# Attention, then routed experts on one core: TensorE's pass regrouped, and x split into f16 parts before its transposes

## The reference

```python
qkv = x @ W_attn + b_attn
q, k, v = jnp.split(qkv, 3, axis=-1)            # 16 heads of 16
scores = jnp.einsum('bhtd,bhsd->bhts', q, k) * scale
scores = jnp.where(causal & (j >= i - 64), scores, -jnp.inf)
out = softmax(scores) @ v
x = layernorm(x + out @ W_proj + b_proj)
...
expert_idx = argmax(softmax(x @ Wr.T))
inter = gelu(x @ W1[expert] + b1[expert])       # 256 -> 1024
y = inter @ Wo + bo + x                         # 1024 -> 256
x = layernorm(x + layernorm(y) * gamma + beta)
```

## Time and profile before

| | us |
|---|---|
| median of 3 runs | 536.47 |
| lowest, highest | 534.67, 536.82 |
| the profiled execution | 537.07 |
| its span (first to last instruction) | 535.3 |
| first transposes of the maxima (pass 0) | 31.95 |
| the same of pass 1, of pass 27, of pass 31 | 42.02, 265.42, 299.76 |

### The profile page before, as it was taken

The page is one execution under the profiler, slowest core; times in us unless marked ns, Lnnn a source line. Parts: engine busy times, 40 slices in busy tenths (PEclk is TensorE's granted clock), DMA queues, the critical chain, the costliest instruction groups (busy, mean ns, idle before and its releaser), DMA issues. The chain is left out here.

```text
span 535.3 us, 24509 instructions
## 1 busy us (share of the span) xinstructions
PE 491.7 (92%) x8576; PEld 434.6 (81%) x8576; DVE 427.2 (80%) x1122; ACT 351.9 (66%) x793; POOL 317.7 (59%) x559
## 2 busy tenths in 40 slices
PE   7799999998999999999977898899999999999980
PEld 6588888877888888888866687788999999999970
DVE  5437978877888888888788647999999989999882
ACT  6246786856686777768676665565676666767850
POOL 8303264535354545546454447777888888888773
PEclk9969999989999999999999899999999999999996
DMA  7797777776877867797762121222235564542100
GB/s 188 210 240 194 216 188 195 206 215 157 216 211 212 234 184 214 210 249 204 199 177 78 52 71 52 71 72 67 66 104 168 194 206 158 170 144 72 50 23 8
DMA packets 90296, 82.28 MB, mean 154 GB/s; under 512 B 36534, under 2 KB 83903, under 8 KB 90050
## 3 DMA queue, kind: packets, MB, share of 16 engines
q1 hardware_dynamic: 86832, 72.26, 49.5%
q0 software_dynamic: 3248, 8.41, 4.6%
q10 hardware_dynamic: 98, 0.04, 0.0%
HBM read 43.50 MB, written 23.55 MB: 125 GB/s over the span
## 5 line engine op out<-in xcount | busy, mean ns | idle before, releaser
L1409 PE MATMUL ps<-v_even,w_hi 128*128 128x128 f16 x1024 | 140.5, 219 | 0.8 <-issue 0.8
L1391 PE MATMUL ps<-wo_hi,ks 128*128 128x256 f16 (+1 forms) x576 | 128.6, 273 | 8.1 <-DVE ks L1087 7.2
L830 ACT ACTIVATE probs<-ps,b1T 128x128 f32<-128x128 f32 (+1 forms) x312 | 85.5, 360 | 67.1 <-PE ps L1409 63.8
L1409 PE MATMUL ps<-v_even,w_lo 128*128 128x128 f16 x512 | 107.9, 219 | 0.0
L1409 PEld LDWEIGHTS ps<-v_even,w_hi 128*128 x1024 | 96.6, 98 | 3.4 <-issue 1.4
L1158 DVE TENSOR_REDUCE mx<-ps 128x4 bf16<-128x512 f32 x128 | 82.6, 683 | 11.9 <-PE ps L1460 11.6
L740 POOL CAST att_hi<-att 128x256 f16<-128x256 f32 x32 | 12.6, 394 | 112.8 <-DVE att L1225 112.8
L1391 PE MATMUL ps<-wo_lo,ks 128*128 128x256 f16 (+1 forms) x288 | 78.5, 273 | 0.0
L1087 DVE TENSOR_TENSOR ks<-probs,ks 128x512 f16<-128x512 f32 (+1 forms) x72 | 69.7, 967 | 8.5 <-ACT ks L837 5.0
L849 ACT ACTIVATE probs<-ps 128x512 f32<-128x512 f32 x128 | 69.5, 611 | 6.7 <-PE ps L1486 3.8
L1509 PE MATMUL ps<-v_odd,probs 128*64 128x17 f32 x1024 | 69.9, 210 | 0.8 <-issue 0.6
(11 more groups left out here) (247 smaller groups left out, 1280.9 us busy)
## 6 DMA issues: line engine op xcount, KB each, us to landing
qk_s<-qk_room SPq DMA_DIRECT2D x32, 256.0 KB, 2.8
w_in<-in_L_ffn_W_dram SPq DMA_DIRECT2D x16, 512.0 KB, 5.7
v_odd<-slots SPq DMA_DIRECT2D x64, 128.0 KB
qs<-qk_s SPq DMA_DIRECT2D x16, 384.0 KB
ks<-qk_s SPq DMA_DIRECT2D x16, 384.0 KB, 5.5
ks<-qk_s SPq DMA_DIRECT2D x32, 144.0 KB
v_even<-v_odd SPq DMA_DIRECT2D x63, 68.0 KB, 3.2
qk_s<-qk_room SPq DMA_DIRECT2D x32, 128.0 KB, 3.0
```

What stands on the lines that cost most here:

```text
L830: last = nc.scalar.activation(g[1 - p][:, ic, n * w:(n + 1) * w], ps_h[1 - p][:, half, col + n * w:col + (n + 1) * w], ACT.Gelu, bias=b1T[ ...
L1391: ins = mm(ps_y[p][0:m], h[p][hs][:, ic, 0:m], wo[ws][:, ic, :], start=n == 0, stop=n == 3 * IC - 1)
L1409: up_ins = mm(ps_h[1 - p][:, half, col + m * w:col + (m + 1) * w], weights(ws, m, k, ic), sT[1 - p][ss][:, k, at], start=k + n == 0, stop= ...
```

## The change

Eight parts:

- On TensorE the output projection and the transposes of x come first, then scores(0) and scores(1), values(0) and the rest (in pass 0 the scores stay first).
- x of the loop (tiles 4 and on) is cut into parts before it is transposed: one pass ahead, ScalarE writes the high f16 part and GpSimd the low one into `part_room`; TensorE makes four f16 transposes of them into bank 4; ScalarE copies both parts out in one instruction. VectorE's `x_low` in the loop goes.
- The tiles `mx` are 128 wide instead of 32, and so is the output of their transposes.
- ScalarE writes the rows of maxima ahead of `v_odd`.
- VectorE computes y and the logits ahead of the maxima, copies att before `router_x`, and does the places ahead of W1.
- W1's halves are two in even passes and none in odd ones, up to pass 28.
- The ranks go to bank 6, but for the last pair, with their wait for v and the router gone; values(0) waits for the places instead.
- Transposes of x no longer wait for the queries and keys of the tile ahead.

```diff
-        mx = [sb(f"mx{k}", [P, P - ALIGNED], bf16) for k in range(2)]
+        mx = [sb(f"mx{k}", [P, P], bf16) for k in range(2)]
...
+        x_part = part_room[:, 0:2 * C].rearrange("p (s c) -> p s c", s=2)
...
+        ps_xT = ps[:, 4, 0:C].bitcast(f16).rearrange("p (s k t) -> p s k t", s=2, k=CC)
...
+        def ps_rank(pair):
+            return ps[:, 6 if pair < TILES // 2 - 1 else 1, 320:320 + 3 * E].rearrange("p (a e) -> p a e", a=3)
...
         def w1_halves(it):
-            halves_at = range(it - 1, it) if it < TILES - 3 else range(2 * it - TILES + 2, 2 * it - TILES + 4)
+            halves_at = range(it - 2, it if it % 2 == 0 else it - 2) if it < TILES - 3 else range(2 * it - TILES + 2, 2 * it - TILES + 4)
...
+                n = it + LEAD + 1
+                if n >= LEAD and a_tile(n):
+                    pool.wait_ge(part_h_done, n - LEAD + 1)
+                    nc.gpsimd.tensor_tensor(x_part[:, 1, :], xin[n % XRING], x_part[:, 0, :], ALU.subtract)\
+                        .then_inc(part_l_done, 1)
                 n = it - 1
                 if a_tile(n):
                     pool.wait_ge(att_done, n + 1)
...
                 for t in turned(it) if it > FIRST else ():
-                    x_high(t)
+                    if t < LEAD:
+                        x_high(t)
+                    else:
+                        act.wait_ge(xT_done, t + 1)
+                        wait(act, v_done, t - 3)
+                        nc.scalar.activation(xT_room[:, 2 * (t % 4):2 * (t % 4) + 2, :],
+                                             ps_xT.rearrange("p s k t -> p s (k t)"), ACT.Copy).then_inc(xl_done, 1)
+                n = it + LEAD + 1
+                if n >= LEAD and a_tile(n):
+                    act.wait_ge(xin_ld[n % 3], 16 * (n // 3 + 1))
+                    nc.scalar.activation(x_part[:, 0, :], xin[n % XRING], ACT.Copy).then_inc(part_h_done, 1)
...
+                cur = a_tile(it)
+                if cur:
+                    act.wait_ge(mxT_done, it + 1)
+                    maxima_rows(0)
+                    maxima_rows(1)
                 if a_tile(it + 1):
                     m = it + 1
                     act.wait_ge(v_done, m + 1)
...
-                maxima(0)
-                maxima(1)
-                for t in turned(it) if it > FIRST else ():
-                    x_low(t)
                 if a_tile(old):
                     dve.wait_ge(proj_done, old + 1)
...
+                maxima(0)
+                maxima(1)
+                for t in turned(it) if FIRST < it < 0 else ():
+                    x_low(t)
...
                 if it == 0:
                     warm(20)
-                scores(0)
+                    scores(0)
+                    scores(1)
                 if a_tile(old):
...
-                    wait(pe, place_done, old // 2)
...
-                scores(1)
                 for t in turned(it):
+                    if t >= LEAD:
+                        pe.wait_ge(part_l_done, t - LEAD + 1)
+                        pe.wait_ge(xl_done, t)
+                        wait(pe, exp_done, 4 * (it - 1) + 1)
+                        for part in range(2):
+                            for k in range(CC):
+                                last = nc.tensor.transpose(ps_xT[:, part, k, :], x_part[:, part, k * P:(k + 1) * P], ident_h[:, :])
+                        last.then_inc(xT_done, 1)
+                        continue
                     pe.wait_ge(xin_ld[t % 3], 16 * (t // 3 + 1))
-                    if t >= LEAD:
-                        pe.wait_ge(qkh_done, t)
-                        pe.wait_ge(qkl_done, t)
...
+                if it != 0:
+                    scores(0)
+                    scores(1)
                 values(0)
```

42 lines of the change are left out of this document (18 added, 24 removed).

## The result

| | before | after |
|---|---|---|
| median, us | 536.64 (534.67 to 538.25, 4 executions) | 547.13 (544.06 to 549.44, 4 executions) |
| profiled execution, us | 537.07 | 549.44 |
| its span, mean granted clock | 535.3, 0.976 | 547.7, 0.942 |
| first transposes of maxima T0, then T1 | 31.95, 42.02 | 33.36, 43.22 |
| T1 to T27 (26 passes) | 223.40 | 231.02 |

The ratio is 1.0166, with an interval of 1.0121 to 1.0212: slower, where 531.0 and faster were forecast, and outside the range of 519.5 to 540. Of the 12.4 us of span, 1.2 are there at T1, 7.6 come in the 26 passes and 3.4 in the last four; the stage behind them is unchanged.

A forecast was written before the change was run, and what follows sets the result against it. TensorE's own length (98% busy) was taken to bound the 26 attention passes. Terms: -6.4 there, -1.2 in the last four passes, +2.1 at the start, sum -5.5 us, median 531.0; forecast 527 to 534, range 519.5 to 540.

The forecast's parts named there:

- Tile shapes and transposes: TensorE's pass: six array-shape changes removed save 0.62 us, f16 transposes of x 0.05; 8.17 falls to 7.50.
- The waits at values(0) and scores(2): TensorE waits 0.30 us for exponentials every pass, 0.24 for a maximum in even ones: passes 7.80 odd, 8.04 even.
- The other 11.0 us are scattered waits that I take to stay: In the 26 attention passes, time beyond 212.4 us of wait-free passes was taken as unchanged: 11.0 us.
- VectorE's chain, worked out for passes with two splits of W1: Even passes: both splits delay the first maximum to T + 5.90, so scores(2) waits 0.24 us; odd passes no wait.
- The last four passes, "-1.2": Last four attention passes: three removed array-shape changes on the path save 0.30 us each pass, -1.2 us.
- The start, "+2.1": Pass -1: ScalarE stands until 25.4 us for tile 4's x, delaying the first maximum and scores(2): +2.1 us, bounds 0 to 4.
- The rival of 545 us, splits of W1 against GpSimd: Even passes: both W1 splits on VectorE collide with GpSimd's work, scores(2) waits 1.08 us more, 13 times: +14.0, 545.0; chance 0.12.
- The full gain, 520: Rival: new waits at values(0) and scores(2) don't arise, TensorE's whole saving arrives: gain 16.5 us, 520.0; chance 0.23.
- The lower end of the range: Whole kernel's time: 519.5 us, described as the middle of the full-gain case, 518 to 526.

The follow-up runs named there:

- mx_first: The changed kernel with VectorE's first two maxima put back ahead of y and the logits: 542.34 us, 1.0107 times the kernel before.
- lock_bad: lock_good with 102 fillers in pass 0 in place of 50, which moves TensorE's instruction fetch boundaries: 551.11 us, 1.032 times the kernel before.
- lock_good: fix4 with small TensorE fillers, 50 in pass 0 and more in odd passes, to hold instruction fetch boundaries in place: 534.51 us, 0.9925 times the kernel before.
- wo_odd: The changed kernel with Wo's four pieces split in passes 15 to 21 instead of 14 to 20: 540.79 us, 1.0044 times the kernel before.
- fix4: The changed kernel with the edits of mx_first and wo_odd, and W1 halves one each in passes 27 and 28: 539.19 us, 1.0049 times the kernel before.
- thin_before: The kernel before with loads of stacked queries and keys cut to an eighth from pair 4 on: 528.45 us, 0.9867 times the kernel before.
- w1_single: The changed kernel with one half of W1 split in every pass instead of two in even passes: 541.08 us, 1.0066 times the kernel before.
- thin_fix4: fix4 with loads of stacked queries and keys cut to an eighth from pair 4 on: 529.16 us, 0.9916 times the kernel before.
- after_again: The changed kernel run once more, nothing altered: 546.0 us, 1.021 times the kernel before.
- thin_after: The changed kernel with loads of stacked queries and keys cut to an eighth from pair 4 on: 534.57 us, 0.9992 times the kernel before.

## Why the prediction was wrong, point by point

- **Tile shapes and transposes** ("TensorE's own pass falls from 8.17 to 7.50"): right. With y behind the maxima an undisturbed pass takes 7.73; the 0.23 above 7.50 are the wait at values(0), forecast as 0.30: in 24 of 26 passes values(0) starts 0.05 us behind the end of the third exponential.
- **The waits at values(0) and scores(2)** (7.80 odd, 8.04 even): right within 0.1. Measured 7.74 and 7.95; mx_first removed the 0.22 of the even passes, which shows where they came from.
- **"The other 11.0 us are scattered waits that I take to stay"**: the step that failed. They became 25.1. Some of those waits were instruction fetches, and in the kernel before they were few: in passes 1 to 26 it has one of 1.00 us and one of 0.65 at a boundary. I had no mechanism for them, and so no reason to hold them fixed. The new order and count of a pass put the boundaries elsewhere against the rest of the pair; in 7 passes TensorE waited 8.0 us there, and these passes lost 14.6, clock included. lock_bad and lock_good show that the place is worth some 14 us by the medians, 18 by the ratios. It is not all: with the places unchanged the waits added up to 3.8 to 10.7 us in nine kernels, so how far the 8.0 belong to the new order and how far to these executions is open.
- **VectorE's chain, worked out for passes with two splits of W1**: the sum left out that Wo's four pieces fall into the same even passes, ahead of y and the maxima. 8.6 us in passes 14 to 20, of which 3.0 were there before; that this queue makes them is shown by the passes of wo_odd, mx_first and fix4. Pass 16 is the exception: it takes 8.9 to 9.0 us in the kernel before, in thin_before, w1_single, wo_odd and thin_fix4 as well, and its cause is open.
- **The clock**: the sum had none of it. The clock was near 1.00 in the earlier trace rows and was taken to stay there, though passes 9 and 10 of that trace had 0.90 and 0.93 around a wait of 1.00 us. In the profile after, it fell to 0.50 behind six of the nine waits of 0.99 us and more in the 26 passes (1.10, 1.10, 1.23, 1.30, 1.36 and 2.00), and stayed at 1.00 behind 0.99, 1.09 and 1.12. In the seven passes of F the loss is 1.8 times the waits (14.6 for 8.0).
- **The last four passes, "-1.2"**: wrong, +3.4. Two splits of W1 in pass 28 took 2.20 us and stood ahead of the table work and y. fix4, without that pair and with the maxima first, brought T27 to T31 to 34.4, the old length, and no gain.
- **The start, "+2.1"**: the mechanism was right (ScalarE stands until 24.95, high part of queries and keys at 25.59 in place of 18.58), the size was 1.4 at T0 and 1.2 at T1. In after_again it was 0.9 and 0.7, in thin_after 3.0 and 2.3, so a single trace does not fix it.
- **The rival of 545 us, splits of W1 against GpSimd**: its time was near, its mechanism was not there. Between T1 and T27 the mean of a split of W1 is 713 ns in both traces. One split of W1 in each trace met GpSimd's addition in full (1.22 us before, 1.13 after), where the rival had two in every even pass. Wo's splits met it in all four of their passes, at 1.14 us each.
- **The full gain, 520**: refuted for this kernel by the wait at values(0), which was there in nearly every pass; no kernel here came near it.
- **The lower end of the range** was said to be the full gain's middle; the middle of 518 to 526 is 522, not 519.5. Nothing hangs on it.

What is settled: Q and F and the clock behind them account for the loss in the 26 passes of the trace, the long waits F stand at boundaries of 256 instructions, and moving the boundaries alone, by one number, moved the time by 14 to 18 us. What makes a boundary cost shows in the packets. At the 68 long waits the packet started 3.9 us (median) behind the boundary before, at the 675 other boundaries 1.8 us. What isn't settled is what delays a packet. DMA bursts have a part (thin loads), the density of instructions near values(1) may have another; no run separates them.

## What to carry to other kernels

Scattered waits without a releaser are a quantity with a mechanism, not a constant: before an order is changed, count the instructions from boundary to boundary and see where the new boundaries fall. When a pass becomes shorter, list everything that stands ahead of the operation that it waits for, also what comes in a few passes only. And price a wait of a microsecond on TensorE at up to twice its length: here some cost their own length alone, and the mean of seven passes was 1.8 times.
